# Where the samples of the expert units are turned, and how they and the features are laid out

## The reference, cut to what matters

```
s0 = relu(x @ swi[0]) @ swo[0];  s1 = relu(x @ swi[1]) @ swo[1]     # 256 -> 1024 -> 256, for all samples
eo = relu(x @ wi[label]) @ wo[label]                                # the sample's own expert
w  = softmax(relu(concat(eo[:, 0], s0[:, 0], s1[:, 0]) @ g1) @ g2)  # three weights a sample
x  = x + eo * w0 + s0 * w1 + s1 * w2
out = x + zX * lap_x(x) + zY * lap_y(x) + zR * x * (1 - x)          # stencil over tokens and features
```

## Time and profile before

| | |
|---|---|
| median of three runs | 1138.02 us |
| profiled execution: its time, its span | 1138.1 us, 1136.6 us |
| PE busy | 1129.7 us, 99% of the span, 5956 matmuls |
| DVE, ACT, POOL busy | 674.2, 456.3, 78.8 us |
| chain that ended last | PE 96%; DVE, SP's queue, DMA 1% each |
| expert stage, shared stage | about 24 to 410 us, 410 to 1137 us |

### The profile page before, as it was taken

How to read it: one execution, slowest core, us unless ns; L and a number is a source line. 1 busy time by engine, 2 the same in 40 slices (tenths; PEclk the granted TensorE clock), 3 DMA queues, 4 the chain that set the end, 5 groups by cost and what they waited for, 6 DMA issues and landing times.

```text
span 1136.6 us, 16584 instructions
## 1 busy us (share of the span) xinstructions
PE 1129.7 (99%) x5956; PEld 962.7 (85%) x5956; DVE 674.2 (59%) x1007; ACT 456.3 (40%) x790; POOL 78.8 (7%) x123
## 2 busy tenths in 40 slices
PE   9999999999999999999999999999999999999998
PEld 8888888888888888888888888888888888888888
DVE  5665667666666635556646555555566465555556
ACT  2554556565565522333333323333333333233233
POOL 1211212111121000000000000000000000000001
PEclk9999999999999999999999999999999999999999
DMA  8555656556665413113023022121130230220200
GB/s 269 174 162 177 190 182 199 180 181 181 177 204 163 115 44 97 24 61 84 19 66 85 11 74 48 47 75 28 58 84 18 66 84 14 72 62 33 75 29 24
DMA packets 111251, 111.82 MB, mean 98 GB/s; under 512 B 78441, under 2 KB 87234, under 8 KB 111170
## 3 DMA queue, kind: packets, MB, share of 16 engines
q1 hardware_dynamic: 96706, 59.58, 19.3%
q0 software_dynamic: 13952, 50.60, 14.8%
q10 hardware_dynamic: 512, 0.59, 0.2%
HBM read 89.40 MB, written 17.04 MB: 94 GB/s over the span
## 4 chain that ended last, share of the span: by engine, by line
PE 96%; DVE 1%; SPq 1%; DMA 1%; issue 0%; ACT 0%; DVEq 0%; ACTq 0%
PE acc L1033 30%; PE hbank L964 15%; PE hbank L965 15%; PE hbank L966 15%; PE acc L1034 15%; SPq L1384 1%; PE tbank L912 1%; PE acc L1019 1%; PE acc L1002 1%; PE hbank L937 0%; DMA rw<-in_L_cond_swi 0%; PE hbank L938 0%; PE acc L1003 0%; PE hbank L980 0%; PE hbank L981 0%
## 5 line engine op out<-in xcount | busy, mean ns | idle before, releaser
L643 DVE SCALAR_TENSOR_TENSOR hl<-hbank,hh 128x512 fp32r<-128x512 f32 (+1 forms) x416 | 271.6, 654 | 410.6 <-ACT hh L1144 410.1
L1144 ACT ACTIVATE hh<-hbank 128x512 fp32r<-128x512 f32 (+1 forms) x416 | 235.7, 568 | 560.3 <-PE hbank L966 557.0
L1033 PE MATMUL acc<-swo,hh 128*128 128x512 f32 x992 | 359.3, 396 | 0.0
L1034 PE MATMUL acc<-swo,hl 128*128 128x256 f32 x992 | 277.8, 280 | 0.0
L1033 PEld LDWEIGHTS acc<-swo,hh 128*128 128x128 f32 x992 | 186.3, 188 | 43.7
L964 PE MATMUL hbank<-xh,swh 128*128 128x512 f32 (+1 forms) x528 | 205.3, 389 | 0.0
L965 PE MATMUL hbank<-xl,swh 128*128 128x512 f32 (+1 forms) x528 | 205.0, 388 | 0.0
L966 PE MATMUL hbank<-xh,swl 128*128 128x512 f32 (+1 forms) x528 | 202.1, 383 | 0.0
L1034 PEld LDWEIGHTS acc<-swo,hl 128*128 128x128 f32 x992 | 187.1, 189 | 9.6
L1033 PE MATMUL acc<-ewo,hh 128*128 128x512 f32 x496 | 180.0, 395 | 0.3 <-DVE hl L643 0.3
L1034 PE MATMUL acc<-ewo,hl 128*128 128x256 f32 x496 | 139.0, 280 | 0.0
(11 more groups left out here) (209 smaller groups left out, 972.4 us busy)
## 6 DMA issues: line engine op xcount, KB each, us to landing
rw<-in_L_cond_wi POOLq DMA_DIRECT2D x44, 512.0 KB, 4.5
rw<-in_L_cond_wo POOLq DMA_DIRECT2D x44, 512.0 KB, 4.8
eo_scratch<-eo SPq DMA_DIRECT2D x128, 64.0 KB, 2.2
xs<-in_x SPq DMA_DIRECT2D x16, 512.0 KB, 4.3
rw<-in_x SPq DMA_DIRECT2D x256, 32.0 KB, 2.2
ei<-eo_scratch SPq DMA_DIRECT2D x16, 512.0 KB, 5.5
xs<-in_x SPq DMA_DIRECT2D x125, 64.0 KB, 3.5
out<-ot SPq DMA_DIRECT2D x15, 512.0 KB, 6.3
```

Of the source, the lines that this page charges most:

```text
L643: e.scalar_tensor_tensor(h_slot(HL, g), bank[:, 0:w], 0.0, h_slot(HH, g).bitcast(F32), ALU.max, ALU.subtract).then_inc(h_lo, 1)
L1033: e.matmul(acc[j][:, 0:2 * D], HH[:, g % NH, js], woc[:, c, :], start=(c == 0), stop=False)
L1034: m = e.matmul(acc[j][:, D:2 * D], HL[:, g % NH, js], woc[:, c, 0:D], start=False, stop=last)
L1144: e.activation(h_slot(HU if upright(g) else HH, g), hbank[g % HRING][:, 0:w], ACT.Relu).then_inc(h_hi, 1)
```

## The change

Samples of units 1 to 21 are now loaded by POOL (`load_samples`, L1314 of the new file), 124 transfers of 64 KB between the loads of weight pieces. Each puts 64 of the 256 features on a group of 32 partitions, in runs of 256 bytes, and DVE's 32 by 32 block transpose turns the whole unit (L623), from which ACT takes the high and DVE the low part (L631), each in one instruction. PE's transposes of these units are gone; unit 0 keeps its own. For this the features are numbered anew: half k of the features is those whose number has bit 5 equal to k, so wi pieces of units from 1 on, and the shared ones, come in two transfers (`piece_loads`). The shared tiles use the same numbering and are loaded in 4 transfers of 256-byte runs in place of 16. Stores of units from 1 on have another shape (`sample_rows`). The rings HH and HL have three places instead of four. Some cuts stand at another chunk.

```diff
-NH = 4
+NH = 3
+NHF = 4
-FIRST_BY = {"ACT": ((1, 0), (1, 1), (1, 2), (1, 3), (2, 0), (2, 1), (2, 2)), "SP": ((1, range(4, 8)), (2, range(3, 8)))}
+FIRST_BY = {"ACT": range(4), "SP": range(4, 8)}
+        _at = (2, 3, 5 if tiny(_n + 1) else 7 if blocks(_n) == 4 else 6)
+    TURN[_n, _at[0]] = HIGH[_n, _at[1]] = LOW[_n, _at[2]] = _tile
+    if tiny(_n + 1):
+        TURN[_n, 6] = HIGH[_n + 1, 0] = LOW[_n + 1, 0] = _tile + 1
...
+    _n, _c = (FIRST - 1, 6) if _t == 0 else (FIRST + 2 * _t - 1, 4)
+    TURN[_n, _c] = HIGH[_n, _c] = LOW[_n, _c + 1] = 1 + NU + _t
...
+        elif blocks(n) == 2:
+            at = {2: (n + 1, 0), 4: (n + 1, 2)}
...
+        def sample_blocks(v, tile, b):
+            return (flat(XS[tile % 2])[:, 128 * b:128 * b + 128],
+                    x[bass.ds(v, 1), :, :].rearrange("z t (a d) -> (z a) t d", d=64))
+        def sample_rows(a, u, b, d, v):
+            if u == 0:
+                return a[b:128:8, :, :], d[bass.ds(v, 1), :, :].rearrange("z (p j) d -> (z p) j d", j=4)
+            return (a[64 * (b % 2):64 * (b % 2) + 64, b // 2, :],
+                    d[bass.ds(v, 1), :, :].rearrange("z (i h) d -> (z h) i d", h=2))
...
+                a = a.rearrange("z (a k e) f -> k (z a) e f", k=2, e=32)
+                return [(to[:, k, :], a[k][:, :, p * 512:(p + 1) * 512]) for k in range(2)]
...
+            def turn_tile(tile):
+                if tile > 2:
+                    e.wait_ge(xt_lo, turned(tile - 1))
+                if tile <= NU:
+                    w = 2 * tile_width(tile)
+                    e.wait_ge(xu_in[tile % 2], XU_VAL[tile])
+                    e.transpose(XZ[:, 0:w], flat(XS[tile % 2])[:, 0:w]).then_inc(xz_done, 1)
+                    return
...
+            def load_samples(u, part):
+                    e.wait_ge(xz_done, turned(tile - 2))
+                for b in range(k)[part]:
+                    e.reg_load(reg, tab[0:1, 0, s0 + b:s0 + b + 1])
+                    v = e.snap(reg, min_val=0, max_val=NS - 1)
+                    e.dma_start(*sample_blocks(v, tile, b)).then_inc(xu_in[tile % 2], 16)
...
+                load_unit(u, (0, 2))
+                    load_samples(u + 1, slice(0, UNITS[u + 1][1] // 2))
+                load_unit(u, (1,))
+                    load_samples(u + 1, slice(UNITS[u + 1][1] // 2, UNITS[u + 1][1]))
+                load_unit(u, (3,))
...
-                    for a in range(4):
-                        e.dma_start(to[32 * a:32 * a + 32, :, 32 * q:32 * q + 32],
-                                    rows[:, :, 32 * a:32 * a + 32]).then_inc(xb_in[t % 2], 16)
+                    rows = x[8 * t + 2 * q:8 * t + 2 * q + 2, :, :].rearrange("b t (a d) -> a (b t) d", d=64)
+                    e.dma_start(to[:, q, :, :], rows).then_inc(xb_in[t % 2], 16)
```

More of the change, by code:

```diff
@@ L106, in tile_parts @@
 def tile_parts(n, c):
[L108 to L121, removed]
+    return [(1, 0), (1, 1)] if (n, c) == (1, 7) else []
 T_ORDER = ["counts"]
@@ L186, in unit_cuts @@
             out.append(at[c])
-    if 3 <= n <= 1 + NU and tiny(n - 1) and c < 2:
+    if 3 <= n <= 1 + NU and blocks(n - 1) < 4 and c < 2:
         out.append((n, 1 + 2 * c))
+    if (n, c) == (3, 0):
+        out.append((3, 3))
     if c == 3 and n - 2 in SHARED_AT:
@@ L331, in cond_resid_program @@
         xb_in = [sem(f"xb_in{i}") for i in range(2)]
+        xu_in = [sem(f"xu_in{i}") for i in range(2)]
         xz_done = sem("xz_done")
@@ L444, in cond_resid_program @@
         X_VAL = {}
-        for tile in range(1 + NU + NT):
-            x_slot[tile % 2] += 16 * (slots_of(tile - 1)[1] if 1 <= tile <= NU else 1)
+        for tile in [0, 1] + list(range(1 + NU, 1 + NU + NT)):
+            x_slot[tile % 2] += 16 * (8 if tile == 1 else 1)
             X_VAL[tile] = x_slot[tile % 2]
+        XU_VAL = {}
+        for tile in range(2, 1 + NU):
+            XU_VAL[tile] = XU_VAL.get(tile - 2, 0) + 16 * UNITS[tile - 1][1]
         st_slot = [0, 0]
@@ L782, in _ @@
                     for tile, k in tile_parts(n, c):
[L783 to L787, removed]
+                        first_low(k)
+                    if (n, c) in LOW:
+                        tile_low(LOW[n, c])
+                    if (n, c) in TURN:
+                        turn_tile(TURN[n, c])
                 if (n, c) == (2, 5):
@@ L832, in _ @@
                         add_x_last(0)
-                if g < G and not tiny(n):
+                if g < G:
                     for ws, p in low_parts_at(n, c):
@@ L892, in slot_rows, with first_transposes @@
                 e.matmul(tbank[0:1, NSLOT:2 * NSLOT], cols[:, 2:3], msel[:], start=True, stop=True).then_inc(t_prod, 1)
[L894 to L899, removed]
-                    e.wait_ge(dve_seq, AT["targets"])
[L902 to L910, removed]
+            def first_transposes(k):
+                if k == 0:
+                    e.wait_ge(x_in[1], X_VAL[1])
+                    e.wait_ge(dve_seq, AT["targets"])
                 for j in range(3):
-                    e.transpose(bank[:, j * 128:(j + 1) * 128], src[:, j, k * 128:(k + 1) * 128], ident[:])
-                e.transpose(bank[:, 384:512], src[:, 3, k * 128:(k + 1) * 128], ident[:]).then_inc(t_prod, 1)
+                    e.transpose(acc[2 + k][:, j * 128:(j + 1) * 128], XS[1][:, j, k * 128:(k + 1) * 128], ident[:])
+                e.transpose(acc[2 + k][:, 384:512], XS[1][:, 3, k * 128:(k + 1) * 128], ident[:]).then_inc(t_prod, 1)
             def gate_hidden():
@@ L946, in first_product @@
                 wh, wl, _ = weights(n)
[L947 to L957, removed]
+                xh, xl = ([half_cols(a, tile, k) for k in range(2)] for a in (XH, XL))
+                to = bank[:, 0:w]
+                if n in HALVES:
+                    js = slice(HALVES[n][0], 4, 2)
+                    xh, xl = ([a.rearrange("p (j n) -> p j n", n=128)[:, js, :] for a in b] for b in (xh, xl))
+                    to = to.rearrange("p (j n) -> p j n", n=128)
+                if c == 0 and tile > 1:
+                    e.wait_ge(xt_lo, turned(tile))
                 if c % 4 == 0:
@@ L1063, in _ @@
                     for tile, k in tile_parts(n, c):
-                        transposes(tile, k)
+                        first_transposes(k)
                 if (n, c) == (2, 5):
@@ L1366, in load_tile_x @@
                 if t < 2:
-                    e.wait_ge(t_prod, T_AT[tile_last(tile - 2)])
+                    e.wait_ge(xz_done, turned(tile - 2))
                 else:
```

228 lines of the change are left out of this document (110 added, 118 removed).

## The result

The changed kernel took 1197.33 us (median of 4 runs, 1188.04 to 1205.36) against 1138.0 us: a ratio of 1.052 with a 95% interval of 1.043 to 1.061. Slower by 59 us where 1124.0 was forecast, and outside the range.

The account below looks back on a forecast made before the run. PE was taken to bound the kernel, busy nearly throughout. From 1138.1 us, 13.3 for transposes, 1.2 for tbank and 0.6 for a wait came off and 1.0 for the gate was added: 1124.0 us, range 1122.2 to 1131.

Parts of the forecast that it names:

- PE's part: Expert stage: PE's unit-tile transposes, the tbank waits and a wait in the last unit's pass go, saving 15.1 us.
- DVE, ACT and three ring places at nothing: Beside PE: tile work fits even the S pass (8.0 of 8.4 us) and three ring places add no wait; cost nothing.
- rival 1: Nine short S and T passes wait 0.5 us each for DVE or ACT: 1128.5 us, chance 0.12.
- POOL's part: POOL's issues at 1.10 us each take 15.4 of a B pass's 22.4 us; sample landings stay hidden; cost 0.
- Rival 3: POOL falls behind issuing samples, as when VectorE locks it out, lengthening B passes: 1169 us, chance 0.05.
- The weights' landing: Weight pieces queued behind samples on POOL start later but still take 4.5 us to land; cost 0.
- The stores' part: Two-engine stores take 1.3 to 1.75 us each, hidden beside B passes; only the gate's load moves, costing 1.0 us.
- Rival 2: Two engines become the bound, ACT waiting for stores of the unit two before: 1173 us, chance 0.13.
- The gate: After the last unit's four stores on SP, the gate's load comes later: 1.0 us, bounds nothing and 2.7 us plus as much again.
- the term that I set to 0: First shared tile's load queues behind a B unit's stores: 0, with 5 us as far end.

Follow-up runs that it names:

- e4: Changed kernel with each unit's store cut in two DMAs of 32 rows and each wi piece as one DMA of outer size 128: 1123.14 us.
- e12: The e4 kernel run once more, in five rounds: 1124.29 us.
- e1: Changed kernel with each unit's store cut in two DMAs of 32 rows, nothing else different: 1145.37 us.
- e7: Kernel before the change with wi and swi pieces on POOL's queue issued as two DMAs of outer size 4: 1138.21 us.
- e2: Kernel before the change with its stores alone changed to outer sizes 16 and 2 (two engines, 4 KB rows): 1147.46 us.
- e13: Kernel before the change with two-engine stores shaped as in the changed kernel (target 2 x 32 x 256, 1 KB rows): 1146.19 us.
- e3: Changed kernel with each wi piece as one DMA of outer size 128, stores left on two engines: 1138.24 us.
- e15: Changed kernel with each sample loaded in one piece, 128 rows of 512 bytes, by POOL; halves and two-engine stores stay: 1142.37 us.
- e5: The e1 kernel with rows of each wi half taken as 16 groups of 8 instead of 4 of 32 (outer size 16): 1125.32 us.
- e6: The e1 kernel with rows of each wi half taken as 8 groups of 16 instead of 4 of 32 (outer size 8): 1127.06 us.
- e10: Changed kernel with stores cut in two DMAs of 32 rows and samples issued by SP, halves at outer size 4: 1220.85 us.

## Why the prediction was wrong, step by step

- **PE's part: right.** I took 15.1 us off. With the DMA side mended, PE is busy 340.00 of 340 us, no transposes of unit tiles are left, and e4 stands 14.1 us below the kernel before on the same chip (1137.27). 1138.1 less 15.1 is 1123.0; e4 and e12 gave 1123.1 and 1124.3. Agreement to the tenth is luck, since e4 and e12 are the same kernel and 1.2 us apart.
- **DVE, ACT and three ring places at nothing: right.** In e4 PE has no wait for DVE or ACT in the nine short passes; rival 1 isn't there.
- **POOL's part: the issue was mis-sized, the sum came out.** The 1.10 us per sample were 1.34, and a weight transfer took 0.71 to 0.80. A B unit takes 8 x 1.34 + 6 x 0.75, 15.2 of 22.4 us, against 15.4 forecast. That two errors cancel is luck. Rival 3 isn't there: no sample's issue took more than 1.37 us in the changed kernel, so a lock-out by VectorE isn't seen. The samples' landing was taken over from another shape too: "2.2 to 3.5 us" were 6.8, and VectorE (L623) waited 11.9 us for them.
- **The weights' landing: the first of two steps that failed.** I kept "take 4.5 us" for the pieces although the change cuts each wi piece into two transfers of outer size 4. I had worked out from the count of short packets that the outer size limits the engines, and applied it to the stores only. On POOL's queue it does something else besides: it adds short packets. They came to 17,664 for the halves and 5,952 for the samples, and pieces landed in 7.7 and 9.5 us. e1 has this failing beside the new samples: 22 us. e7 shows that late landings (7.5 and 8.4 us) are hidden in the kernel before, whose POOL queue has no samples between the pieces.
- **The stores' part: the second. The mechanism was seen, the price wrong.** "A store takes 1.3 to 1.75 us, eight 10 to 14 us beside 22.4 us of pass: still hidden." One rate was read at a DMA share of 0.22. The other was read at full queues, but it is what all queues together got from an engine, not what the stores get beside POOL's queue. In the changed kernel twelve stores in a row took 56 us, 4.7 us each, the last landed 24.77 us after its issue, and SP stood 5.76 us in the issue ahead of it. e2 and e13 show that such stores are hidden where nothing else of the change is there: no new wait in 340 us. e3 has this failing beside the new samples: 15 us.
- **Either step would have been enough.** e1, e3 and e15 each have one of the three ingredients mended, and at 1138 to 1145 us all three lie outside the forecast's 1122.2 to 1131. The prediction priced each edit by itself and had no term for what they cost together, about half of the 74 us.
- **Rival 2 named the place,** ACT before taking a unit out, for the unit two before, at a chance of 0.13. Its 1173 us for 1197 came near by luck: it summed megabytes over a whole stage on engines 0 and 1. By that sum e3, with the same stores, samples and bytes, would lose 49 us too; it loses 15.
- **The gate: +1.0 us forecast, 3.7 measured** in e3 and in the changed kernel (DMA e<-eo_scratch above). It was inside the bounds given. In e2 the first shared tile's blocks, behind the stores on SP's queue, make VectorE wait 7.1 us (3.7 before) and PE 3.6 us, beside 3.9 for the gate. That is the term that I set to 0, with 5 us as far end; in e3 no such wait shows.
- **PE's clock: no term for it.** The spans of the changed kernel and of e4 differ by 63.7 us. 45.1 are waits in the expert stage and 3.7 the gate; the other 15 go with a lower clock, granted 0.83 and 0.94 where PE stood waiting and 1.00 where not (mean 0.981). For the same 5832 matmuls PE is busy 1130.6 us in the changed kernel and 1116.0 in e4.

The Trainium skill (DMA: Bandwidth & Descriptors, on why a DMA increments its semaphore by 16) gives the rule for the number of engines, and for POOL's queue adds that k consecutive engines are taken from a cursor that goes round, while hardware queues take the lowest. The packets agree on the hardware side: each of the 120 stores of e3 has 30 packets fewer than its two in e4 (62,498 - 58,898 = 3,600), which is 2 completions instead of 32. That narrow transfers of POOL load all the engines in turn would fit the share of 0.94 in the stall. No run here shows which engine a packet took.

Open: how an engine shares its time between POOL's queue and SP's, and so why a store takes 24.8 us when the engines are 94% busy. The runs show that the ingredients cost about twice as much together as the sum of what each costs alone, not by what rule. Nor do they show why 4 KB packets take longer beside short ones. Of the 74 us, I also can't say how much is the samples' 256-byte runs, how much their 48 short packets each, and how much the 0.8 us more of POOL's time for each issue; e15 removes all three.

## What to carry to other kernels

Work out for every DMA that a change adds or cuts up the smaller outer size of its two sides, above all on GpSimd's queue, and don't take its landing time over from the shape before. Watch the DMA share of the windows, not the bytes: this kernel went from 0.58 to 0.74 with fewer bytes a second. With stores on all engines at most 2 us were lost at a share of 0.73 (e5, e7), 4 at 0.85 (e6) and 22 at 0.93 (e1). And when several edits draw on the same engines, don't price them one by one: here 15 and 22 us made 74.

## What the runs showed of the hardware

- On GpSimd's queue a transfer with k engines (outer size k = 4, 8, 16) left its data packets times 16/k plus 16 packets: 272, 144 and 80 for 256 KB. The added ones were of 8 bytes (halves, 11 ns each) or 64 (samples). On SP's queue a store of k = 2 left 2 completions and no fill.
- At equal throughput (180 and 179 GB/s) the busy share of the DMA engines rose from 0.67 (e4) to 0.93 (e1) when the wi pieces came as halves of outer size 4. Most of the added time was in GpSimd's 4 KB packets, 286 ns each for 218.
- SP's issue of a 64 KB DMA, 0.5 to 0.6 us at the median, stretched to 5.8 us (changed kernel, a store) and 7.7 us (e10, a sample); the issues behind it waited too. With 32 KB a store on all engines and whole pieces (e4) nothing of the kind made anyone wait.
- GpSimd's issue of a 64 KB load took 1338 ns as 4 x 64 x 64 elements with 256-byte runs and 538 ns as 128 rows of 512 bytes.
- VectorE's block transpose read pairs of columns apart (every second element) in e4 in the same 1239 ns for 128 x 1024 as contiguous columns in the changed kernel.
